# Projection two chunks ahead, one buffer per part, the first normalisation recomputed, and the mamba weights loaded in projection

## The reference

```
xn  = layernorm(x)                       # mean and variance of each row of 256
out = x + mamba(xn) + ffn(xn)

mamba(xn): xc, res = split(xn @ W_in)    # 256 -> 512 + 512
           xs = silu(conv_b + sum_j shift(xc, j) * conv_w[:, j])    # 4 taps, causal
           dt, B, C from xs; scan over the rows with 16 states per channel
           (y * silu(res)) @ W_out
ffn(xn):   hn = layernorm(xn) * g1 + b1  # a second normalisation of the rows
           q, k, v = hn @ wq + bq, hn @ wk + bk, hn @ wv + bv
           attention with 16 heads of 16; x1 = xn + o @ wo + bo
           hn2 = layernorm(x1) * g2 + b2; the best of 8 experts for each row
           x1 + expert(hn2)
```

## Time and profile before

| | us |
|---|---|
| median of three runs | 3468.39 |
| the profiled execution, its own time | 3471.77 |
| its span on the core | 3470.2 |
| projection, start to the first instruction of mamba | 220.9 |
| mamba's first product | 238.0 |
| attention's first product | 1426.0 |

### The profile page before, as it was taken

The page is one execution under the profiler, slowest core; times in us unless marked ns, Lnnn a source line. Parts: engine busy times, 40 slices in busy tenths (PEclk is TensorE's granted clock), DMA queues, the critical chain, the costliest instruction groups (busy, mean ns, idle before and its releaser), DMA issues. The chain is left out here.

```text
span 3470.2 us, 42850 instructions
## 1 busy us (share of the span) xinstructions
PE 2911.1 (84%) x12668; PEld 1388.7 (40%) x12668; DVE 2599.9 (75%) x3764; ACT 1710.9 (49%) x2099; POOL 927.4 (27%) x527
## 2 busy tenths in 40 slices
PE   5768697897987967699999999998999997439998
PEld 3333243343433423333333333333333332438887
DVE  5526898998998999588898888888989993552222
ACT  2324545545545454066676666666767777101110
POOL 2203554554645655300000000000000000234443
PEclk9878899998998988599998999999999999669999
DMA  4542121112211111745544545554454520336663
GB/s 147 163 141 80 62 73 61 74 68 72 79 55 68 68 64 39 98 64 84 84 60 67 77 63 84 66 80 78 59 81 58 63 39 18 115 80 210 199 204 123
DMA packets 218020, 300.78 MB, mean 87 GB/s; under 512 B 117906, under 2 KB 162476, under 8 KB 203346
## 3 DMA queue, kind: packets, MB, share of 16 engines
q1 hardware_dynamic: 205298, 268.27, 35.1%
q0 software_dynamic: 12512, 29.82, 2.9%
HBM read 245.37 MB, written 57.60 MB: 87 GB/s over the span
## 5 line engine op out<-in xcount | busy, mean ns | idle before, releaser
L736 DVE TENSOR_REDUCE attn_mx<-attn_pX 128x1 f32<-128x512 f32 x2048 | 1271.1, 682 | 183.7 <-PE attn_pX L642 181.8
L714 ACT ACTIVATE attn_pr<-attn_pS 128x1024 f32<-128x1024 f32 x1024 | 992.7, 1022 | 525.3 <-PE attn_pS L655 525.1
L642 PE MATMUL attn_pX<-attn_ks,attn_qs 48*128 48x512 f32 x2048 | 754.7, 495 | 75.1 <-DMA attn_vs<-v_d 25.2
L1186 PE MATMUL mamba_pY<-mamba_g,mamba_ident 128*128 128x512 f32 x1024 | 530.4, 667 | 203.7 <-DVE mamba_g L1312 203.1
L1299 DVE TENSOR_TENSOR_SCAN mamba_h<-mamba_pA,mamba_hs,mamba_db 128x512 f32<-128x512 f32 x512 | 617.6, 1263 | 66.2 <-ACT mamba_pA L1045 65.6
L642 PEld LDWEIGHTS attn_pX<-attn_ks,attn_qs 48*128 48x128 f32 x2048 | 307.7, 192 | 776.9 <-DVE attn_mx L736 713.0
L982 POOL TENSOR_TENSOR mamba_db<-mamba_bq,mamba_u 128x2048 f32<-128x2048 f32 x128 | 579.3, 4526 | 73.1 <-DVE mamba_u L1259 72.8
L1045 ACT ACTIVATE mamba_pA<-mamba_dt,mamba_an 128x512 f32<-128x512 f32 x512 | 351.7, 691 | 497.8 <-DVE mamba_h L1299 497.5
L665 PE MATMUL attn_pO<-attn_pr,attn_vs 128*17 128x512 f32 x4096 | 557.5, 617 | 0.4 <-ACT attn_pr L714 0.4
L655 PE MATMUL attn_pS<-attn_qs,attn_ks 50*128 50x512 f32 x2048 | 473.5, 418 | 51.4 <-DMA attn_qs<-attn_mt 30.8
L1186 PEld LDWEIGHTS mamba_pY<-mamba_g,mamba_ident 128*128 128x128 f32 x1024 | 213.2, 214 | 504.2 <-DVE mamba_g L1312 259.9
(11 more groups left out here) (185 smaller groups left out, 2052.3 us busy)
## 6 DMA issues: line engine op xcount, KB each, us to landing
mamba_bq<-bc_d SPq DMA_DIRECT2D x64, 1024.0 KB, 4.7
attn_ks<-parts_d SPq DMA_DIRECT2D x192, 256.0 KB, 8.9
exp_w<-in_w SPq DMA_DIRECT2D x46, 1024.0 KB, 5.5
attn_vs<-v_d SPq DMA_DIRECT2D x32, 544.0 KB, 15.5
parts_d<-proj_qp SPq DMA_DIRECT2D x32, 512.0 KB, 3.0
attn_qs<-parts_d SPq DMA_DIRECT2D x192, 64.0 KB, 8.3
attn_qs<-attn_mt SPq DMA_DIRECT2D x512, 1.0 KB
oraw_d<-attn_oe SPq DMA_DIRECT2D x32, 256.0 KB, 2.1
```

The lines of the kernel that those rows point to most:

```text
L642: pe.matmul(pX[bank(s, n)][:, :], QS[slot][rows, pair, qt * P:(qt + 1) * P], KS[slot][rows, pair, part * BANK:(part + 1) * BANK], start=Tr ...
L714: act.activation(PR[2 * (kt % 2) + pair][:, :, :], pS[pair][:, :, :], ACT.Exp, scale=HD ** -0.5).then_inc(p_sb, 1)
L736: dve.tensor_reduce(MX[:, col:col + 1], pX[bank(s, n)][:, :], AX.X, ALU.max).then_inc(x_max, 1)
L1186: mm = pe.matmul(pY[j][:, :], ident[:, :], G[k % 2][:, n, :], start=False, stop=(q == NQ - 1 and n == QN - 1))
```

## The change

In projection the rows have three buffers, the loads go first on GpSimd, and all norm work for chunk c+2 is done by VectorE while chunk c is projected; before the first product two chunks are normalised. There is one QP buffer for each of the four parts, and VS holds a whole chunk, twice. The bias of the values is no longer a product but an addition by GpSimd over the chunk (`value_bias`), and four stores per chunk follow it. The loops are written out. xn_d is gone: mean and reciprocal deviation of each row stay in SBUF (mv1, rstd1), and in attention GpSimd makes the normalised rows anew from x, by two operations of 128 x 1024 more per chunk and one load less. Mamba's weights live in buffers allocated before projection; SyncE loads them after projection's own weights, and GpSimd makes the taps in projection, two per chunk in chunks 2 to 5. The core of the diff:

```
-        X = [m.sb(f"x{s}", [P, TG, C]) for s in range(2)]
+        X = [m.sb(f"x{n}", [P, TG, C]) for n in range(RX)]
         HN = [m.sb(f"hn{s}", [P, TG, C]) for s in range(2)]
         ST = m.sb("stats", [P, TG, 6])
         MV = m.sb("meanvar", [P, TG, 2])
         V, ROOT, R, TMP = (m.sb(n, [P, TG]) for n in ("var", "root", "rstd", "tmp"))
+        WC = mamba_w[0]
+        TAPS, DI = conv_w.shape
+        CW = m.sb("cw", [P, TAPS, DI])
...
-        TR = [[m.sb(f"tr{s}{n}", [P, KC, BANK]) for n in range(2)] for s in range(2)]
+        TX = [m.sb(f"tx{s}", [P, KC, BANK]) for s in range(2)]
+        TH = [m.sb(f"th{s}", [P, KC, BANK]) for s in range(2)]
-        BV = m.sb("bv", [1, C])
-        ONE = m.sb("one", [1, P])
+        BV = m.sb("bv", [P, C])
         QF = [m.sb(f"qf{n}", [P, BANK]) for n in range(2)]
-        QP = [m.sb(f"qp{n}", [P, 2, BANK], F32R) for n in range(2)]
-        VS = [m.sb(f"vs{n}", [P, HEADS, VW]) for n in range(2)]
+        QP = [m.sb(f"qp{r}", [P, 2, BANK], F32R) for r in range(4)]
+        VS = [m.sb(f"vs{s}", [P, TG, HEADS, VW]) for s in range(2)]
...
             def _(pool):
+                def load_x(c):
+                    if c >= RX:
+                        pool.wait_ge(x_turned, KC * (c - RX + 1))
+                        pool.wait_ge(hn_raw, c - RX + 1)
+                    pool.dma_start(X[c % RX][:, :, :], x[c * BANK:(c + 1) * BANK, :].rearrange("(t p) c -> p t c", p=P)
+                                   ).then_inc(x_in[c % RX], 16)
+                def scale(c):
+                    pool.wait_ge(hn_raw, c + 1)
+                    pool.tensor_tensor(HN[c % 2][:, :, :], HN[c % 2][:, :, :],
+                                       G[:, :].unsqueeze(1).to_broadcast([P, TG, C]), ALU.mult).then_inc(hn_mul, 1)
+                    pool.wait_ge(hn_mul, c + 1)
+                    pool.tensor_tensor(HN[c % 2][:, :, :], HN[c % 2][:, :, :],
+                                       B[:, :].unsqueeze(1).to_broadcast([P, TG, C]), ALU.add).then_inc(hn_done, 1)
+                def value_bias(c):
+                    pool.wait_ge(v_sb, TG * (c + 1))
+                    v = VS[c % 2][:, :, :, 0:HD]
+                    pool.tensor_tensor(v, v, BV[:, :].rearrange("p (h d) -> p h d", d=HD).unsqueeze(1)
+                                       .to_broadcast([P, TG, HEADS, HD]), ALU.add).then_inc(v_done, 1)
...
+                for c in range(RX):
+                    load_x(c)
                 make_identity(pool, ident, id_ready)
                 pool.wait_ge(w_in, 16 * 8)
+                scale(0)
+                scale(1)
+                def tap(n):
+                    k, a = divmod(n, TAPS)
+                    a = TAPS - 1 - a
+                    pool.tensor_tensor(WC[:, k, a, :], WC[:, k, 0, :], CW[:, a, :], ALU.mult).then_inc(wc_done, 1)
+                for c in range(NCH):
+                    if c + RX < NCH:
+                        load_x(c + RX)
+                    value_bias(c)
+                    if c == 2:
+                        pool.wait_ge(mamba_ld, 16 * (len(mamba_w) + 1))
+                    if 2 <= c < 2 + KC * TAPS // 2:
+                        tap(2 * (c - 2))
+                        tap(2 * (c - 2) + 1)
+                    if c + 2 < NCH:
+                        scale(c + 2)
...
             def _(sp):
+                for dst, src in ((BV, bv), (G, g1), (B, b1)):
+                    sp.dma_start(dst[:, :], bcast_rows(src, P)).then_inc(w_in, 16)
+                sp.dma_start(WC[:, :, 0, :], mamba_in[0]).then_inc(mamba_ld, 16)
+                for dst, src in zip(mamba_w[1:], mamba_in[1:]):
+                    sp.dma_start(dst, src).then_inc(mamba_ld, 16)
+                sp.dma_start(CW[:, :, :], conv_w.rearrange("(o k) d -> o k d", o=1).to_broadcast([P, TAPS, DI])
+                             ).then_inc(mamba_ld, 16)
...
+                def store_values(c):
+                    sp.wait_ge(v_done, c + 1)
+                    b, cb = divmod(c, NB)
+                    for g in range(GB):
+                        sp.dma_start(v_d[b * GB + g, cb * BANK:(cb + 1) * BANK, :].rearrange("(t p) x -> p t x", p=P),
+                                     VS[c % 2][:, :, g * GH:(g + 1) * GH, :].rearrange("p t h x -> p t (h x)")
+                                     ).then_inc(v_out[c % 2], 16)
+                for c in range(NCH):
+                    store_turned(c)
+                    store_part(c, 0)
+                    store_part(c, 1)
+                    store_part(c, 2)
+                    store_part(c, 3)
+                    store_values(c)
+                sp.wait_ge(wc_done, KC * TAPS)
...
             def _(pe):
+                def values(c):
                     for t in range(TG):
+                        if TG * c + t >= 2:
+                            pe.wait_ge(v_sb, TG * c + t - 1)
                         for kk in range(KC):
+                            mm = pe.matmul(pV[t % 2][:, 0:C], TH[c % 2][:, kk, t * P:(t + 1) * P], WV[:, kk, :],
+                                           start=(kk == 0), stop=(kk == KC - 1))
+                        mm.then_inc(v_ps, 1)
+                pe.wait_ge(id_ready, 2)
+                turn(0)
+                pe.wait_ge(w_in, 16 * 8)
+                for c in range(NCH):
+                    queries_keys(c)
+                    if c + 1 < NCH:
+                        turn(c + 1)
+                    values(c)
...
             def _(act):
+                def split(c, r):
+                    qk, k = divmod(r, KC)
+                    act.wait_ge(qk_ps, 4 * c + r + 1)
+                    if 4 * c + r >= 2:
+                        act.wait_ge(qk_low, 4 * c + r - 1)
+                    act.activation(QF[r % 2][:, :], pQ[r % 2][:, :], ACT.Identity, bias=BQK[:, qk, k:k + 1]
+                                   ).then_inc(qk_f, 1)
+                    if c >= 1:
+                        act.wait_ge(parts_out[r], 16 * c)
+                    act.activation(QP[r][:, 0, :], pQ[r % 2][:, :], ACT.Identity, bias=BQK[:, qk, k:k + 1]
+                                   ).then_inc(qk_hi, 1)
+                def copy_values(c):
+                    if c >= 2:
+                        act.wait_ge(v_out[c % 2], 16 * GB * (c // 2))
+                    for t in range(TG):
+                        act.wait_ge(v_ps, TG * c + t + 1)
+                        act.copy(VS[c % 2][:, t, :, 0:HD], pV[t % 2][:, 0:C].rearrange("p (h d) -> p h d", d=HD)
+                                 ).then_inc(v_sb, 1)
...
+                copy_turned(0)
+                for c in range(NCH):
+                    split(c, 0)
+                    split(c, 1)
+                    if c + 2 < NCH:
+                        root(c + 2, 0)
+                    split(c, 2)
+                    split(c, 3)
+                    if c + 1 < NCH:
+                        copy_turned(c + 1)
+                    if c + 2 < NCH:
+                        root(c + 2, 1)
+                    copy_values(c)
...
             def _(dve):
+                for c in range(2):
+                    first_norm(c)
+                    second_norm(c)
+                    scaled_rows(c)
+                copy_turned(0)
+                for c in range(NCH):
+                    if c + 2 < NCH:
+                        first_norm(c + 2)
+                    low(c, 0)
+                    low(c, 1)
+                    if c + 2 < NCH:
+                        second_norm(c + 2)
+                    low(c, 2)
+                    low(c, 3)
+                    if c + 1 < NCH:
+                        copy_turned(c + 1)
+                    if c + 2 < NCH:
+                        scaled_rows(c + 2)
...
-                    for dst, src in ((XN[c], xn_d), (XB[c], x), (MOB, mo_d)):
+                    for dst, src in ((XB[c], x), (MOB, mo_d)):
                         pool.dma_start(dst[:, :, :], src[rows, :].rearrange("(t p) c -> p t c", p=P)).then_inc(x_in, 16)
-                    pool.wait_ge(x_in, 48 * (c + 1))
+                    pool.wait_ge(x_in, 32 * (c + 1))
+                    mean = mv1[:, c * TG:(c + 1) * TG, 0].unsqueeze(2).to_broadcast([P, TG, C])
+                    rstd = rstd1[:, c * TG:(c + 1) * TG].unsqueeze(2).to_broadcast([P, TG, C])
+                    pool.tensor_tensor(XN[c][:, :, :], XB[c][:, :, :], mean, ALU.subtract).then_inc(x_done, 1)
+                    pool.wait_ge(x_done, 3 * c + 1)
+                    pool.tensor_tensor(XN[c][:, :, :], XN[c][:, :, :], rstd, ALU.mult).then_inc(x_done, 1)
+                    pool.wait_ge(x_done, 3 * c + 2)
                     pool.tensor_tensor(XN[c][:, :, :], XN[c][:, :, :], BO[:, :].unsqueeze(1).to_broadcast([P, TG, C]),
                                        ALU.add)
                     pool.tensor_tensor(XB[c][:, :, :], XB[c][:, :, :], MOB[:, :, :], ALU.add).then_inc(x_done, 1)
-                    pool.wait_ge(x_done, c + 1)
+                    pool.wait_ge(x_done, 3 * c + 3)
...
```

(47 more changed lines are left out.)

340 lines of the change are left out of this document (129 added, 211 removed).

## The result

The changed kernel takes 3416.8 us (median of 4 runs, 3412.6 to 3419.8), the kernel before on the same chip 3466.8 (4 runs, 3464.8 to 3471.9): the ratio is 0.9853, 95% interval 0.9835 to 0.9870. The forecast of 3414 was 3 us off and 3394 to 3436 held it. The profiled execution took 3419.8 us (span 3418.1), 52.0 less than the one of before.

What follows compares the result with a forecast made beforehand. Projection was taken to be held by round trips of stores and row loads, with no engine full. Mamba starting 42.6 us earlier and its start 12.1 shorter make -54.7 from 3468.4: 3414 us, range 3394 to 3436.

Steps and rivals of the forecast that it cites:

- Pace of a chunk: Projection loop: VectorE's work and the port held by GpSimd give 18.0 us a chunk, 19.5 with taps.
- GpSimd's hold: Projection: GpSimd's operations hold VectorE on the shared port, 0.7 us at the first subtraction and 1.8 at the value bias.
- The wait for the products: Projection: VectorE's subtractions wait for TensorE's query products, so a chunk takes 15.5 us with nothing held, against 13.2 of work.
- The sum by full addition: Projection: all of GpSimd's 7.0 us added to VectorE's 13.2, at most 20.2 us a chunk without taps.
- Rivals 1: Projection: the port hardly costs, chunks of 15.5 us, 17 us more gain, total 3397 us; chance 0.13.
- 2 (22): Projection: GpSimd's work adds fully, five chunks of 22 us, 15.5 us less gain, total 3429 us; chance 0.17.
- The round trip: Old projection loop: ScalarE waits 57.2 us for value stores, VectorE 44.6 for new rows, and TensorE waits behind VectorE.
- hidden: Projection: GpSimd's load of chunk c+4, queued behind bias, taps and scaling, is needed over a chunk later and costs nothing.
- Start, tail, mamba's start: Projection's first product at 32 us, 5 later; its tail 20 us, from 23.7; mamba's own start 12.1 us shorter.
- rival 3: Projection: transfers hold the loop, so its pace stays and only mamba's start is won, total 3456 us; chance 0.04.
- Attention: Attention stage: two more GpSimd operations and one load less per chunk change its time by 0 us, bounds -2 and +8.
- Rival 4: Attention: less idle time in projection lowers TensorE's granted clock later; at 0.91 it costs 62 us, total 3476; chance 0.03.

Runs made afterwards that it cites:

- rx2: The changed kernel with two row buffers in projection in place of three; ratio 1.0002 to the kernel before.
- rows_stored: The changed kernel with normalised rows again stored in projection and loaded in attention, GpSimd recomputing nothing; ratio 0.9864 to the kernel before.
- f2_pad: The changed kernel with twelve 0.5 MB loads, each waited for, between projection and mamba; one execution, mamba starts at 221.1 us, attention takes 1470 us.

## Why the prediction was right, step by step

*Pace of a chunk.* Right in kind, and near in size partly by luck: 16.8 for 18.0, 18.7 for 19.5, 14.7 for 16.1. Two terms were off in opposite directions. GpSimd's hold I had at 2.5 us (0.7 and 1.8); it lengthens VectorE's instructions by 4.55 and the chunk by 3.8. The wait for the products I had at 2.3 (15.5 with nothing held, against 13.2 of work); with GpSimd's arithmetic gone the chunk took 13.0, since I had placed the subtractions by query products of 10.07 us, and they take 7.13 now. My sum of VectorE's work, 13.2, was too high as well: 11.75. The first scaling falls on the statistics, as I had it, and costs 0.5 us; the second and the bias addition hold VectorE for most of their length (3.43 in place of 1.38, 2.11 in place of 0.16). The pair of taps costs 1.9, not 1.5. The Trainium skill (SBUF — State Buffer, SBUF's two separate sides) has the lock for the whole instruction; the pair at 79.84 and 79.92 agrees, 2.11 in place of 0.16. The sum by full addition, 20.2, does not come about: 16.8 was measured. Rivals 1 (15.5) and 2 (22) lie on either side of what came.

*What bounded the kernel before.* The round trip was the right kind of thing, but I put its largest part at the v_d stores, whose 57.2 us I had vanish. The rx2 kernel has no such wait and the old pace: two row buffers are enough to hold the changed loop at 26 us, through the order of GpSimd's queue. Whether the old loop, whose order is another, was held by its row ring alone is not shown. My expectation for rx2 failed for the same reason, since I counted the load's 4 us and not what stands ahead of it. The prediction passed that load by with one word, "hidden", where the third buffer turned out to be what the loop's gain hangs on.

*Start, tail, mamba's start.* Copies of chunk 0 at 29.57 (30.4); t of chunk 6 at 133.95 (141); queries of chunk 7 19.2 us later (17.2); tail 21.6 (20): from the last v_d issue's end, 168.5, to mamba 6.2 us pass, not 4.9. Mamba starts at 174.7 (178.3), its product follows 3.7 us later (5.0). Sum -59.7 against -54.7.

*Transfers (rival 3).* Refuted: the pace of the loop did change, and the rows_stored kernel moves 0.5 MB a chunk more at the same pace.

*Attention.* The step that failed. I took 0 with bounds of -2 and +8, and thought of VectorE's small steps; 14.9 us were lost, and 19 in the mean of eight profiles with GpSimd's bias against four with TensorE's (1474.1 and 1454.8). Rival 4 had the place and the sign, a lower granted clock in attention, but not the cause (less idle time ahead: f2_pad speaks against it) nor the size, since a hundredth of the clock came and not four; the prediction's own price, 15 us for each hundredth, fits the 14.9. What lowers the clock there stays open. The test that I set, the same length behind mamba's first product within 5 us, came out at 3239.7 for 3232.2. That the total was met within 3 us is luck: this loss of 14.9 stood against 5.0 us more in front of mamba, 2.6 in mamba and the 4.8 by which the part behind attention varied.

## What to carry to other kernels

The longest wait in a list need not bound the loop: follow the load on which a chunk starts, with all that is queued ahead of its issue, and see that it has a buffer to itself (25.9 us a chunk without, 16.8 with it). Work moved to GpSimd beside a busy VectorE costs half to three quarters of its length (3.8 of 7.0 us, 1.9 of 2.55); an operation that VectorE can do in a copy that it makes anyway (scale and offset after the turn, 0.12 us more for each of two copies) is nearly free. A gain in one stage is checked on the stages behind it, with the clock of each, over several profiles: here 10 to 17 of the 60 us were lost again there.

## What the runs showed of the hardware

VectorE's small steps and subtractions stood behind a GpSimd operation until it ended (2.11 us in place of 0.16, 3.43 in place of 1.38), and its statistics did not (1.39). The stretches at half clock came at nearly the same places of attention in 14 profiles, while their lengths differed (86 to 151 us in all). Between the profile of before and that of the changed kernel taken again, attention lengthens by about half of the added half-clock time (107 to 141 us, 1457.4 to 1475.9 us). I had not expected the group of a kernel to go with where the values' bias is added, 1200 us earlier; no run shows why.
